# Attention 1 of a gated decoder block: row maxima carried as a 49th row of the score product, values split into two weight tiles with three products, and the lower exponentials shared by DVE and GpSimd

## What is computed

```
scores = einsum('bshd,bthd->bhst', q, k) / sqrt(8)
p      = softmax(where(mask & causal, scores, -inf))
x      = x + tanh(gate) * (einsum('bhst,bthd->bshd', p, v) @ w_o.T + b_o)
```

## Time and profile before

| | us |
|---|---|
| runs, median (lowest, highest) | 1551.35 (1550.51, 1555.36) |
| the profiled execution | 1554.9 |
| its span in the trace | 1553.1 |
| mean granted TensorE clock, share of 2.4 GHz | 0.949 |
| TensorE busy | 1379.2 |
| DVE busy | 1207.5 |
| ACT busy | 1011.5 |
| POOL busy | 769.1 |

### The profile page before, as it was taken

The page is one execution under the profiler, slowest core; times in us unless marked ns, Lnnn a source line. Parts: engine busy times, 40 slices in busy tenths (PEclk is TensorE's granted clock), DMA queues, the critical chain, the costliest instruction groups (busy, mean ns, idle before and its releaser), DMA issues. The chain is left out here.

```text
span 1553.1 us, 30256 instructions
## 1 busy us (share of the span) xinstructions
PE 1379.2 (89%) x11712; PEld 1181.4 (76%) x11712; DVE 1207.5 (78%) x2349; ACT 1011.5 (65%) x2152; POOL 769.1 (50%) x788
## 2 busy tenths in 40 slices
PE   0677999999999999999999986999689898894995
PEld 0667999999999999999999974777346555553995
DVE  8799888888988888888888896433359887876554
ACT  4897777887778778877787754211146664562773
POOL 5776656565565665665654442001123433332672
PEclk9799999999999999999999998999779998985997
DMA  3100100000001001000010003320452002003553
GB/s 103 55 19 17 35 15 15 22 15 15 22 15 34 3 15 35 15 15 22 15 52 1 1 1 128 57 35 21 94 81 58 14 2 68 1 15 136 192 208 129
DMA packets 62238, 69.84 MB, mean 45 GB/s; under 512 B 5424, under 2 KB 54800, under 8 KB 61968
## 3 DMA queue, kind: packets, MB, share of 16 engines
q1 hardware_dynamic: 59488, 60.54, 14.7%
q0 software_dynamic: 2432, 7.34, 1.4%
q10 hardware_dynamic: 176, 0.04, 0.0%
HBM read 55.56 MB, written 12.34 MB: 44 GB/s over the span
## 5 line engine op out<-in xcount | busy, mean ns | idle before, releaser
L880 POOL TENSOR_TENSOR RB<-YS,M 128x512 bf16<-128x512 f32 x128 | 161.5, 1261 | 246.2 <-DVE YS L739 246.2
L566 ACT ACTIVATE QT<-B,sm 128x256 f32<-128x256 f32 x256 | 131.9, 570 | 165.4 <-PE B L423 165.4
L443 PE MATMUL SS<-QT,KT 128*128 128x256 f32 x512 | 154.9, 397 | 10.6 <-DVE mx L694 10.5
L1748 POOL TENSOR_SCALAR_AFFINE_SELECT P<-P 128x1024 f32<-128x1024 f32 x64 | 81.6, 1275 | 160.0 <-ACT P L1602 160.0
L876 POOL TENSOR_TENSOR yy<-vv,half 128x12 f32<-128x12 f32 x64 | 148.4, 2318 | 5.3
L391 PE MATMUL PA<-WH,XQ 128*128 128x256 f32 x512 | 140.8, 307 | 5.0 <-ACT SQ L595 5.0
L393 PE MATMUL PA<-WL,XQ 128*128 128x256 f32 x512 | 129.7, 284 | 0.0
L713 DVE TENSOR_TENSOR QN<-QN,yy 128x512 f32<-128x512 f32 x128 | 124.4, 972 | 2.2 <-POOL yy L876 2.2
L694 DVE TENSOR_REDUCE mx<-SS 128x4 bf16<-128x512 f32 x128 | 87.9, 687 | 42.9 <-PE SS L435 41.9
L706 DVE TENSOR_REDUCE vv<-SQ 128x6 f32<-128x768 f32 x128 | 120.5, 941 | 0.0
L411 PE MATMUL PA<-W,XB 128*128 128x128 bf16 x1536 | 109.4, 221 | 2.6 <-POOL XB L817 2.6
(11 more groups left out here) (328 smaller groups left out, 4471.9 us busy)
## 6 DMA issues: line engine op xcount, KB each, us to landing
W<-in_w SPq DMA_DIRECT2D x16, 1024.0 KB, 7.9
Q<-qsc SPq DMA_DIRECT2D x48, 128.0 KB
WR<-in_wprojT SPq DMA_DIRECT2D x16, 256.0 KB, 2.9
K<-ksc SPq DMA_DIRECT2D x12, 256.0 KB
qsc<-T POOLq DMA_DIRECT2D x8, 384.0 KB, 4.2
X<-in_x SPq DMA_DIRECT2D x4, 512.0 KB, 5.9
CR<-in_xctxT SPq DMA_DIRECT2D x8, 256.0 KB, 3.0
RSM<-rsm_d SPq DMA_DIRECT2D x16, 128.0 KB, 4.3
```

The costliest lines, as they stand in the source:

```text
L443: pe.matmul(SS[:, 256 * z:256 * z + 256], k[:, 128 * z:128 * z + 128], q[:, 256 * z:256 * z + 256], start=True, stop=False)
L566: a.activation(QT[i % 2][:, o:o + 256], B1[:, o:o + 256], ACT.Identity, bias=col(n + "b"), scale=col(n + "w"))
L880: p.tensor_tensor(RB[i % 2][:], YS[:], M[:], ALU.subtract).then_inc(s_rb, 1)
```

## The change

1. **Maxima as a 49th row.** The maxima of a sequence's four units are gathered in one tile (32 columns), turned once per sequence by one product (`pe_max_turn`), copied to SBUF as bf16 by ACT (`act_max_turned`), and written by two DMAs (`sp_maxima`) into partition 48 of each half of Q6. Partition 48 of each half of K6 is filled with ones by a DMA before the stage. The score product then has 49 rows and the eight products of line 1482 are gone.
2. **Longer pipeline.** The maxima of a whole sequence must be there before its first shifted product, so `pe_shifted_1`, `act_expo_1` and `pool_select` move from unit n-2 to unit n-7, `act_upper` and `dve_lower` from n-3 to n-8, `pe_weigh_1` from n-4 to n-9; all later work moves by five steps, the loop from 78 to 81 steps. Transposes and logits of the next layer are spread over other steps of the TensorE stream.
3. **Values as weights in two parts.** VPH and VPL hold the upper and lower parts of the values; each group has three products (upper x upper, lower x upper, upper x lower) that sum in PSUM, six products of 512 columns per unit in place of four. DVE's copy and addition in the normalisation go.
4. **Lower exponentials shared.** DVE forms the first 256 columns of each half, GpSimd the other 256 (`pool_lower`), each 128 x 512 elements.
5. **Bias.** The bias is added to x by GpSimd (`pool_bias`), once per sequence, in place of DVE's second operation in `dve_residual_1`.
6. In the feed-forward stage the split of the values (lines 1256 and 1351) is gone.

```diff
         def sp_attention_1(sp):
...
             for q4 in range(4):
                 sp.wait_ge(s_qst[q4], 32)
                 for half in range(2):
                     for z in range(NP):
...
                         sp.dma_start(Q6[r0:r0 + 8, :, 512 * q4:512 * q4 + 512], src[...]).then_inc(s_qg[q4], 16)
-            for n in range(N1 + 14):
+            for n in range(N1 + 17):
+                b = every(n, 4, 5, NB)
+                if b is not None:
+                    sp_maxima(sp, b)
                 if n == 40:
...
+        def sp_maxima(sp, b):
+            sp.wait_ge(s_mte, b + 1)
+            for half in range(2):
+                sp.dma_start(Q6[64 * half + 48:64 * half + 49, :, 128 * b:128 * b + 128],
+                             MT[b % 2][16 * half:16 * half + 16, :]).then_inc(s_mr[b % 2], 16)
...
+        def pe_max_turn(pe, b):
+            pe.wait_ge(s_mx, N + 4 * b + 4)
+            if b:
+                pe.wait_ge(s_mte, b)
...
+            pe.matmul(SS[0:32, 256:384], mxb[b % 2][:], negib[:], start=True, stop=True).then_inc(s_mt, 1)
+
         def pe_shifted_1(pe, i):
-            pe.wait_ge(s_mx, N + i + 1)
+            if i % 4 == 0:
+                pe.wait_ge(s_mr[b % 2], 32 * (b // 2 + 1))
             if i:
                 pe.wait_ge(s_ex, N + i)
-            for n in range(8):
-                pe.matmul(STB[:, 128 * n:128 * n + 128], mx1[i % 2][:, n:n + 1].broadcast_to([128, 128]), negib[:], ...)
             for half in range(2):
-                r = slice(64 * half, 64 * half + 8 * NP)
+                r = slice(64 * half, 64 * half + 8 * NP + 1)
...
         def pe_weigh_1(pe, i):
...
+                pe.wait_ge(s_lo2 if g2 else s_lo1, i + 1)
-                pe.matmul(ps_[:], vp[:, o:o + 128], PH1[i % 2][:, :, n], start=g % 4 == 0, stop=False)
-                t = pe.matmul(ps_[:], vp[:, o:o + 128], PL1[i % 2][:, :, n], start=False, stop=g % 4 == 3)
+                pe.matmul(OT[u % 2][:], vh[:, o:o + 128], PH1[i % 2][:, :, n], start=g % 4 == 0, stop=False)
+                pe.matmul(OT[u % 2][:], vl[:, o:o + 128], PH1[i % 2][:, :, n], start=False, stop=False)
+                t = pe.matmul(OT[u % 2][:], vh[:, o:o + 128], PL1[i % 2][:, :, n], start=False, stop=g % 4 == 3)
...
+        def act_max_turned(a, b):
+            a.wait_ge(s_mt, b + 1)
...
+            a.activation(MT[b % 2][:], SS[0:32, 256:384], ACT.Copy).then_inc(s_mte, 1)
...
         def dve_lower(v, i):
+            v.wait_ge(s_up1, i + 1)
+            v.tensor_tensor(PL1[i % 2][:, :, 0:256], P1[i % 2][...][:, :, 0:256], PH1[i % 2][:, :, 0:256], ALU.subtract)...
+        def pool_lower(p, i):
+            p.wait_ge(s_up1, i + 1)
+            p.tensor_tensor(PL1[i % 2][:, :, 256:512], P1[i % 2][...][:, :, 256:512], PH1[i % 2][:, :, 256:512], ALU.subtract)...
...
         def pool_attention_1(p):
-            for n in range(N1 + 14):
+            for n in range(N1 + 17):
                 if n == 40:
                     pool_routing_constants(p)
-                b = every(n, 4, 0, NB)
+                b = every(n, 4, 4, NB)
                 if b is not None:
                     pool_values(p, b)
-                if 0 <= n - 2 < N1:
-                    pool_select(p, n - 2)
+                b = every(n, 4, 6, NB)
+                if b is not None:
+                    pool_bias(p, b)
+                if 0 <= n - 8 < N1:
+                    pool_lower(p, n - 8)
+                if 0 <= n - 7 < N1:
+                    pool_select(p, n - 7)
                 if n in NEXT and NEXT[n] <= 2:
                     pool_layer_root(p, 3, NEXT[n])
```

More of the change, by code:

```diff
@@ L1039, in sp_feed_forward_0 @@
             sp.wait_ge(s_ks, 64)
+            sp.wait_ge(s_vone, 2)
             for half in range(2):
+                sp.dma_start(K6[64 * half + 48:64 * half + 49, :, :].rearrange("o g (b t) -> o (g b) t", t=128),
+                             ones1[:]).then_inc(s_kg, 16)
                 for z in range(NP):
@@ L1175, in act_keys_values @@
             a.wait_ge(s_kv, q4 + 1)
[L1176 to L1179, removed]
+            a.activation(VS[:, 4 * q4:4 * q4 + 4, :, 0:8], PAh[1][:, 0:256].rearrange("p (b g d) -> p b g d", g=G, d=8),
+                         ACT.Copy).then_inc(s_kvr, 1)
         def act_last_turn(a):
@@ L1362, in pool_feed_forward_0 @@
             pool_parts(p, 1)
-            for z in range(2):
-                p.memset(VS[:, :, :, 8 + 9 * z:9 + 9 * z], 1.0 - z).then_inc(s_vone, 1)
+            p.memset(VS[:, :, :, 8:9], 1.0).then_inc(s_vone, 1)
+            p.memset(ones1[:], 1.0).then_inc(s_vone, 1)
             p.memset(caus[:], 0.0).then_inc(*ps.up())
@@ L1512, in pe_turn_1 @@
             pe.wait_ge(s_rt, N + u + 1)
-            if u % 2 == 0 and b:
-                pe.wait_ge(s_oe, b)
+            if u % 2 == 0:
+                pe.wait_ge(s_mte, min(b + 2, NB))
+                if b:
+                    pe.wait_ge(s_oe, b)
             if u % 2 and b:
@@ L1517, in pe_turn_1 @@
             if u % 2 and b >= 5:
-                pe.wait_ge(s_lg, b - 4)
+                pe.wait_ge(s_xt, b - 4)
+            if u % 2 and b >= 6:
+                pe.wait_ge(s_lg, b - 5)
             for j in range(4):
@@ L1584, in pe_attention_1 @@
                     pe_raw(pe, n)
-                b = every(n, 4, 28, NB - 4)
-                if b is not None:
-                    pe_next_turn(pe, b)
             for b in range(NB - 4, NB):
@@ L1617, in act_out_turn @@
                 a.wait_ge(s_C, N + b)
-            a.activation(AOT[:].rearrange("p c n -> p (c n)"), TR[0][:, 0:256], ACT.Copy).then_inc(s_oe, 1)
+            a.activation(AOT[:].rearrange("p c n -> p (c n)"), SS[:, 0:256], ACT.Copy).then_inc(s_oe, 1)
         def act_next_turn(a, b):
@@ L1626, in act_attention_1 @@
             after_feed_forward_0(a)
-            for n in range(N1 + 14):
-                u = every(n, 2, 6, 2 * NB)
+            for n in range(N1 + 17):
+                b = every(n, 4, 5, NB)
+                if b is not None:
+                    act_max_turned(a, b)
+                u = every(n, 2, 11, 2 * NB)
                 if u is not None:
                     act_evac_out(a, u)
-                b = every(n, 4, 10, NB)
+                b = every(n, 4, 15, NB)
                 if b is not None:
                     act_out_turn(a, b)
-                if 0 <= n - 3 < N1:
-                    act_upper(a, n - 3)
-                if 0 <= n - 2 < N1:
-                    act_expo_1(a, n - 2)
-                b = every(n, 4, 28, NB - 4)
+                if 0 <= n - 8 < N1:
+                    act_upper(a, n - 8)
+                if 0 <= n - 7 < N1:
+                    act_expo_1(a, n - 7)
+                b = every(n, 4, 33, NB - 4)
                 if b is not None:
@@ L1815, in build @@
         s_out = sem("out")
[L1820 removed]
+        F24, F16 = 4 * NI, NB
         def bc(ap):
```

175 lines of the change are left out of this document (91 added, 84 removed).

## The result

The changed kernel takes 1598.56 us (median of 4 runs, 1587.2 to 1612.25), beside 1550.93 for the kernel before (4 runs, 1547.86 to 1555.36). The ratio is 1.028, 95% interval 1.022 to 1.034: slower, by 43 us by this ratio and by 47.6 by the medians. Medians here are of all executions of a kernel, while ratios leave out executions over 1.5% above its fastest. Its profiled execution is the shortest of the four: 1587.2 us, span 1585.2, against 1554.9 and 1553.1. Three stretches give the 32.1 us between the two spans, but for rounding: the first exponentials of attention 1 come 23.3 us later, the loop from the first to the last exponentials is 11.3 longer, and what follows is 2.5 shorter.

What follows compares the result with a forecast made beforehand. It took a ring of ACT and POOL work in attention 1 as the bound, with TensorE and DVE nearly equal. Start +47, loop +18 and tail -2 gave +63: 1551 + 63 = 1614 us, range 1578 to 1640.

Steps and rivals of the forecast that it cites:

- Start, +47: Attention 1's first exponentials at 1185.0 against 1138.1, as the maxima DMAs queue behind 48 loads: +47 us (+41 to +49).
- Ring of 4.0: Attention 1 loop: upper part, POOL's lower, select, upper part again; one turn 4.0 us against 3.3 to 3.5.
- rival A: Loads in the way, but DVE's and POOL's subtractions out of step: ring 3.46, turns 3.6, total 1580; chance 0.22.
- Stalls of 21: Attention 1 loop: time above smooth turns, from rounds 11, constants 2, scaling 3, zeroing and clock 5; 39 before.
- Loop +18: Attention 1, first to last exponentials: 252 us of turns plus 21 of stalls, 273 against 255.1, +18.
- Tail -2: Four tail steps after the last unit: DVE's normalisations and residuals get shorter, -2 us.
- TensorE at 3.2 to 3.5 per unit: Attention 1 loop: TensorE needs 3.2 to 3.5 us of each 4.0 turn, net -0.2, which earns nothing.
- B: Rival: TensorE idles in the longer turns and its clock falls; turns of 4.4, loop +38, total 1634; chance 0.13.
- C: Rival: the maxima overtake the loads, start only +2, the collision of DVE and POOL stays; total 1569; chance 0.08.
- D: Rival, faster: the maxima overtake the loads and DVE and POOL are out of step; total 1535; chance 0.05.
- E: Rival: no effect, gain and loss cancel; needs a mean turn of 3.3 with the late start; chance 0.02.

Runs made afterwards that it cites:

- experiment 3: Changed kernel with 12 loads of Q6 ahead of the first maxima and the other 36 in parts behind later maxima; 1573.64 us, ratio 1.015.
- experiment 4: Changed kernel with the two maxima DMAs issued by ACT on its own queue instead of SP, all loads still ahead in SP's stream; 1587.36 us, ratio 1.021.
- experiment 1: The changed kernel timed again without any edit; 1603.99 us, ratio 1.038 to the kernel before.
- experiment 6: Changed kernel with DVE's half of the lower part cut to 8 of 256 columns per half from unit 2 on; 1586.89 us, one execution.
- experiment 7: Changed kernel with POOL's select placed ahead of its lower part; 1596.72 us, ratio 1.026.
- experiment 5: Changed kernel with the whole lower part formed by DVE, none by POOL; 1585.08 us, six runs in two groups, ratio 1.014 from the faster group.
- experiment 8: Changed kernel with loads in parts, whole lower part by DVE, POOL's cast of values two steps later and bias three; 1547.43 us, ratio 0.997.
- experiment 9: As experiment 8, plus POOL's three layer norm rounds spread behind the selects of three steps and DVE's scaling two steps later; 1538.30 us, ratio 0.990.

## Why the prediction was right in kind, and where its sizes were off

The forecast was slower, 1614 us with a range of 1578 to 1640; the median came at 1599, inside its own range (1598 to 1630) by a hair. By its steps:

- **Start, +47: right mechanism, wrong size.** That the maxima stand in SP's stream behind the loads is shown by the rows at 1152.48 and 1159.38 and by experiments 3 and 4. The term was +23.3 in the profiled execution. What was off is "SP issues those from 1102.73 to 1176.90": it took one execution's 74.17 us for a constant. It is 49.6 to 78.8, from one trace to the next. With 60.08 the first exponentials came at 1171.96 (+34), with 78.81 at 1195.44 (+57). The landing, 6 us behind the last issue, was 6.9 here (1152.48 to 1159.38), but 11.1, 12.2, 13.6 and 16.0 in the four other traces with this order (experiments 1, 6, 7 and 5): it too grows as the loads move more slowly. So the forecast's one number should have carried a range of some 35 us here (+23 to +57), not of 8.
- **Ring of 4.0: right.** 3.99 measured. POOL's lower at 1.75 was 1.77, and its two parts, 1.20 alone and 0.55 by the collision, were 1.26 and 0.51 (experiment 6). That both halves start on one signal held in all smooth turns (1200.68 and 1200.73), which refutes "out of step" (rival A's turn of 3.6). The Trainium skill (GPSIMD Engine Reference, Engine selection) has two-input work about twice as slow on GpSimd; the rows make it 1.26 against 0.69, a factor of 1.8, between the row's 1.20 that the sum used and the 1.38 by the rule. The choice of 1.20 was 0.06 per turn low, and the collision 0.04 high.
- **Stalls of 21: somewhat too high.** 15.1. The turns at the rounds lie 2.6 to 2.7 above the smooth one where 3.7 was put, 8 in all for 11: POOL's wait for DVE's statistics, 2.83 before, was 0.77. The constants, put at 2, cost 2.5. The turns three after the rounds cost 4.6 where 3 were put down to the scaling; what ends ACT's wait in them is the product that turns the maxima, a wait for which the prediction had no term. The 5 set aside for the zeroing of `eout` and for TensorE's steps at the lower clock show in one turn of 4.61 alone; whether the 0.50 from 1256 to 1260 lengthens the turn of 4.93 was not separated.
- **Loop +18: +11.3**, from the stalls (-6) and 63 turns of 3.99 for 4.0. **Tail -2: -2.5.** TensorE at 3.2 to 3.5 per unit was no bound: it is busy 225 us of the loop's 266, before 232 of 255.
- **The rivals.** B (turns of 4.4 at a lower clock) fell: the smooth turns are 3.99, and the granted clock is 0.94 on average over the loop. C and D needed maxima that overtake the loads; in the change's order they don't, while by ACT's queue they land in 8 us (experiment 4). E fell. D's other half, a ring back at 3.30 with no late start, is experiment 8, and it gave 0.3% and not D's 1%: before, 47 us of the loop lay above 63 turns of 3.30, and in experiment 8 36 still do. A gain beyond that came only when POOL's rounds were spread as well (experiment 9).

By the medians the change costs 47.6 us in the first comparison and 57.0 in experiment 1; the profiled executions, with two of the shorter series of loads, show 32.1 and 44.2, split as above.

## What to carry to other kernels

Before half of an operation moves to an idle engine, look at what stands behind it in that engine's stream: here 1.26 us of POOL and 0.51 of collision went in ahead of the select, a member of the ring, and POOL's busy share of 50% had said nothing about it. A small transfer that starts a pipeline must not stand behind bulk loads in the same engine's stream; put the loads in parts behind it, and take the duration of a long series of loads from several executions before it enters a sum. When a tight ring has been relieved, look next at what else stands in its members' streams, here POOL's rounds and ACT's wait for the turned maxima, and spread it: the rounds gave 9 of the 14 us by which the last version beats the kernel before, though in the kernel before the same edit lost 7.

## What the runs showed of the hardware

- The same 48 DMAs, 128 KB each, issued in a row by SP into 8 partitions each, took 49.6 to 78.8 us to issue from one execution to the next, with or without other engines at work (78.64 with attention held back, 74.17 and 64.93 with it running). The DMA engines' busy share is 0.55 or 0.56 whether they move 157 GB/s or 70, and a transfer issued last in the series was waited for 6.9 to 16.0 us. Twelve alone took 8.4 to 9.0 us, and later ones in groups of 6, with pauses, 2.3 a group.
- A DVE subtraction of two operands and a GpSimd one that start together cost GpSimd 0.51 us of DVE's 0.69 (1.77 against 1.26). If DVE comes second, both it and the select behind it are longer, 1.15 for 0.69 and 1.54 for 1.09 (one turn of the changed kernel):

```profile
1259.31 1.27 POOL L1790 TENSOR_TENSOR PL<-P,PE 128x512 fp32r<-128x512 f32 x1 [1.18 <-ACT PE L1639]
...
1259.97 1.15 DVE L1691 TENSOR_TENSOR PL<-P,PE 128x512 fp32r<-128x512 f32 x1
...
1260.54 1.54 POOL L1785 TENSOR_SCALAR_AFFINE_SELECT P<-P 128x1024 f32<-128x1024 f32 x1
```

Whichever of POOL's two operations meets DVE's half, the turn stays near 4.0 (3.95 there). In experiment 7 DVE's half starts 0.13 us before POOL's subtraction ends, and both keep their own length, 0.69 and 1.29.
